# Head-wise weighted values in half-height tiles, with the sums of weights moved and inverted through DRAM

## What is computed

```
xn = _layernorm(x, axis=-1)
x = x + attn(xn, Wqkv, Wout) + ffn(xn, W1, b1, W2, b2)      # ffn: relu(xn W1 + b1) W2 + b2, 256 -> 1024 -> 256

# attn: H = 16 heads of hd = 16, segments of 512 tokens, keys are every 8th token of a segment (64 keys)
scores = jnp.einsum('bhspd,bhskd->bhspk', q4, k4)            # 512 x 64 for each head and segment
c = jnp.max(scores, axis=4, keepdims=True)                   # over blocks of 64 tokens, per key
w = jnp.exp(scores - c)
den = jnp.sum(w, axis=-1) + 1e-10
num = jnp.einsum('bhsnmk,bhskd->bhsnmd', w, v4)
out = num / den[..., None]                                   # then times Wout
```

## Time and profile before

| | |
|---|---|
| time, median of 3 runs | 1187.57 us (1187.46 to 1188.78) |
| profiled execution, span (the page gives no other time for it) | 1189.4 us |
| TensorE busy | 1162.9 us, 98% |
| VectorE busy | 885.6 us, 74% (reciprocals 222.3 us of it) |
| ScalarE, GpSimd busy | 657.1 us (55%), 613.5 us (52%) |
| 16 DMA engines | 32.6% |

### The profile page before, as it was taken

The page is one execution under the profiler, slowest core; times in us unless marked ns, Lnnn a source line. Parts: engine busy times, 40 slices in busy tenths (PEclk is TensorE's granted clock), DMA queues, the critical chain, the costliest instruction groups (busy, mean ns, idle before and its releaser), DMA issues.

```text
span 1189.4 us, 22871 instructions
## 1 busy us (share of the span) xinstructions
PE 1162.9 (98%) x7457; PEld 955.7 (80%) x7457; DVE 885.6 (74%) x1437; ACT 657.1 (55%) x1142; POOL 613.5 (52%) x488
## 2 busy tenths in 40 slices
PE   5799999999999999999999999999999999999998
PEld 3578888888878888888888888888888888888888
DVE  7788777778787777777777787777877777777762
ACT  4545555565655565555565555556555555555653
POOL 2435654465554455554556544556544556544554
PEclk9889999999999999999999999999999999999999
DMA  5423343222333322333222433223343233332210
GB/s 184 99 73 93 85 106 100 63 82 70 101 101 84 80 72 81 98 106 84 68 81 75 106 101 84 72 70 88 101 106 82 56 87 84 106 102 55 67 49 36
DMA packets 75402, 102.24 MB, mean 86 GB/s; under 512 B 13808, under 2 KB 42096, under 8 KB 75376
## 3 DMA queue, kind: packets, MB, share of 16 engines
q1 hardware_dynamic: 75376, 101.90, 32.6%
HBM read 22.16 MB, written 16.78 MB: 33 GB/s over the span
## 4 chain that ended last, share of the span: by engine, by line
PE 96%; DVE 1%; issue 0%; SPq 0%; POOL 0%; DMA 0%; ACT 0%; DVEq 0%; POOLq 0%
PE y_bank L690 39%; PE h_bank L690 38%; PE misc L811 5%; PE s_bank L742 5%; PE misc L814 5%; PE misc L756 2%; PE misc L690 2%; PE misc L781 0%; PE misc L764 0%; DMA q_pack<-q_hi 0%; PE s_bank L690 0%; DVE w_exp L589 0%; DVE s_max L583 0%; DVE xn_keys L544 0%; DVE w_lo L506 0%
## 5 line engine op out<-in xcount | busy, mean ns | idle before, releaser
L338 POOL TENSOR_TENSOR h_lo<-h_full,h_hi 128x512 fp32r<-128x512 f32 x256 | 336.7, 1318 | 557.2 <-ACT h_full L403 553.3
L409 ACT ACTIVATE w_exp<-w_exp 128x512 f32<-128x512 f32 x256 | 162.7, 636 | 238.7 <-DVE w_exp L589 238.7
L690 PE MATMUL y_bank<-w_hi,h_hi 128*128 128x256 f32 x1024 | 290.6, 284 | 0.0
L690 PE MATMUL y_bank<-w_lo,h_hi 128*128 128x256 f32 x1024 | 290.5, 284 | 0.0
L690 PE MATMUL y_bank<-w_hi,h_lo 128*128 128x256 f32 x1024 | 290.2, 283 | 0.0
L596 DVE RECIPROCAL den<-den 128x256 f32<-128x256 f32 x128 | 222.3, 1739 | 39.9 <-ACT den L422 39.9
L401 ACT ACTIVATE h_hi<-h_bank,b_cols 128x512 fp32r<-128x512 f32 x256 | 176.1, 688 | 82.6 <-PE h_bank L690 76.8
L690 PE MATMUL h_bank<-xt_hi,w_hi 128*128 128x512 f32 x512 | 210.8, 412 | 1.9 <-DVE q_lo L611 1.9
L690 PEld LDWEIGHTS y_bank<-w_lo,h_hi 128*128 128x128 f32 x1024 | 196.0, 191 | 9.9
L690 PEld LDWEIGHTS y_bank<-w_hi,h_hi 128*128 128x128 f32 x1024 | 195.5, 191 | 9.3
L690 PE MATMUL h_bank<-xt_lo,w_hi 128*128 128x512 f32 x512 | 201.9, 394 | 0.0
(11 more groups left out here) (91 smaller groups left out, 1708.1 us busy)
## 6 DMA issues: line engine op xcount, KB each, us to landing
q_pack<-q_hi SPq DMA_DIRECT2D x256, 128.0 KB, 2.4
x_raw<-x SPq DMA_DIRECT2D x32, 512.0 KB, 3.3
q_pack<-q_lo SPq DMA_DIRECT2D x128, 128.0 KB, 2.4
out<-y SPq DMA_DIRECT2D x32, 512.0 KB, 2.9
k_pack<-k_hi SPq DMA_DIRECT2D x256, 32.0 KB, 1.9
k_pack<-k_lo SPq DMA_DIRECT2D x128, 32.0 KB, 1.9
x_keys<-x SPq DMA_DIRECT2D x16, 128.0 KB, 3.0
w_exp<-w SPq DMA_DIRECT2D x2, 1024.0 KB, 8.8
```

The lines of the kernel that those rows point to most:

```text
L338: pool.tensor_tensor(h_part[1][:, i % HBUF], h_full[:, i % HBUF], f32(h_part[0][:, i % HBUF]), ALU.subtract).then_inc(h_lo, 1)
L409: act.activation(w_exp[:, pair], w_exp[:, pair], ACT.Exp).then_inc(w_ready, 1)
L690: mm = pe.matmul(ps, stationary[a], moving[b], start=start and c == 0 and n == 0, stop=stop and c == len(pairs) - 1 and n == 2, skip_group ...
```

## The change

The change computes the same. Weighted values and sums of weights come out of one set of products: `v` holds for each pair 32 columns in which values and ones alternate, and each head has a product of its own, with its 64 keys as rows and 32 columns: 8 products for a quad, head a = 0 of the pairs into `misc[0]` and a = 1 into `misc[1]`. So every second row of a bank is a value row, and the others all hold a sum. ACT takes both banks in one copy of 128 x 1024. SP moves one sum row of each head (4 rows a bank) to DRAM and reads them back as 128 x 64; DVE adds 1e-10 and inverts that; SP writes it to DRAM again and reads it back into the 64 rows of each half in four DMAs; another DMA merges the value rows of the second bank into the first. POOL multiplies. Wout is loaded with its rows in the new order, in four DMAs. Cut to its core:

```diff
-        v = sb("v", [P, 2, D], F32)
+        v = sb("v", [P, 2, PAIRS, PW], F32)
...
@@ SyncE
+            def move_den(s):
+                sp.wait_ge(num_den_ready, (s + 1) * QUADS)
+                for a in range(2):
+                    sp.dma_start(den_dram[:, :, a].rearrange("q j n -> j q n"),
+                                 num_den[1 - a::PW, :, a]).then_inc(den_out, 16)
+                sp.wait_ge(den_out, (s + 1) * 32)
+                sp.dma_start(den[:], den_dram.rearrange("q j a (c n) -> (q j a c) n", c=P // H)).then_inc(den_in, 16)
+                sp.dma_start(num_den[1::2, :, 0], num_den[1::2, :, 1]).then_inc(num_merged, 16)
+            def move_rden(s):
+                sp.wait_ge(rden_ready, s + 1)
+                sp.dma_start(rden_dram.rearrange("q j a (c n) -> (q j a c) n", c=P // H), rden[:]).then_inc(rden_out, 16)
+                sp.wait_ge(rden_out, (s + 1) * 16)
+                for quad in range(QUADS):
+                    for a in range(2):
+                        sp.dma_start(rden_rows[a::2, quad],
+                                     rden_dram[quad, :, a].unsqueeze(1).to_broadcast([P // PW, HD, SEG])
+                                     ).then_inc(rden_rows_in, 16)
             def step(s, par, ffn, attention, norm, load):
+                if ffn:
+                    move_rden(s)
                 if load:
...
                 if norm:
                     pack(s)
+                if attention:
+                    move_den(s + 1)
                 if ffn:
                     sp.wait_ge(y_ready, (s + 1) * YB)
@@ GpSimd
             def attention_out(s, quad):
-                pool.wait_ge(rden_ready, (s * QUADS + quad + 1) * (RP // QUADS))
-                pool.wait_ge(num_ready, s * QUADS + quad + 1)
+                pool.wait_ge(rden_rows_in, (s + 1) * 64)
+                pool.wait_ge(num_merged, (s + 1) * 16)
...
-                    if i in (4, 6) and ffn:
-                        attention_out(s, i // 2 - 2)
-                    if i in (5, 7) and ffn:
-                        attention_lo(s, i // 2 - 2, par)
+                    if i in (6, 7) and ffn:
+                        attention_out(s, i - 6)
+                if ffn:
+                    for quad in range(QUADS):
+                        attention_lo(s, quad, par)
@@ ScalarE
-                act.copy(num[:, quad], misc[0][:]).then_inc(num_ready, 1)
-                act.add(den[:, quad], misc[1][:], GUARD).then_inc(den_ready, 1)
+                act.copy(num_den[:, quad], misc_banks[:]).then_inc(num_den_ready, 1)
...
-                    if i == 5 and ffn:
-                        attention_hi(s, 0, par)
...
                 if ffn:
+                    attention_hi(s, 0, par)
+                if attention:
+                    exponential(s, PAIRS - 2)
+                if ffn:
                     attention_hi(s, 1, par)
-                if attention:
-                    exponential(s, PAIRS - 2)
@@ VectorE
-                dve.reciprocal(den[:, quad, columns], den[:, quad, columns]).then_inc(rden_ready, 1)
+            def invert_den(s):
+                dve.wait_ge(den_in, (s + 1) * 16)
+                dve.tensor_scalar(den[:], den[:], GUARD, None, ALU.add).then_inc(den_guarded, 1)
+                dve.wait_ge(den_guarded, s + 1)
+                dve.wait_ge(rden_out, past(s * 16))
+                dve.reciprocal(rden[:], den[:]).then_inc(rden_ready, 1)
...
-                    if n in (2, 4) and ffn:
-                        invert_den(s, RP // QUADS + n // 2 - 1)
+                    if n == 2 and ffn:
+                        invert_den(s)
...
@@ TensorE, weighted_values
-                for j, pair in enumerate(pairs):
-                    pe.matmul(misc[0][PW * j:PW * (j + 1), :], v[:, 1 - par, PW * pair:PW * (pair + 1)],
-                              w_exp[:, pair], start=True, stop=True)
-                for j, pair in enumerate(pairs):
-                    mm = pe.matmul(misc[1][PW * j:PW * (j + 1), :], head_ones[:], w_exp[:, pair],
-                                   start=True, stop=True)
+                for j in range(PAIRS // QUADS):
+                    pair = quad * (PAIRS // QUADS) + j
+                    for a in range(2):
+                        rows = slice(a * KEYS, (a + 1) * KEYS)
+                        mm = pe.matmul(misc[a][PW * j:PW * (j + 1)], v[rows, 1 - par, pair], w_exp[rows, pair],
+                                       start=True, stop=True)
```

More of the change, by code:

```diff
@@ L128, in bank @@
             return ctx.enter_context(nc.psum_tensor(name, [P, SEG], F32))
-        misc = [bank(f"misc{i}") for i in range(2)]
+        misc_banks = ctx.enter_context(nc.psum_tensor("misc", [P, 2, SEG], F32))
+        misc = [misc_banks[:, i] for i in range(2)]
         h_bank = [bank(f"h_bank{i}") for i in range(2)]
@@ L180, in ln_attention_ffn @@
         pv_psum = sem("pv_psum")
-        num_ready = sem("num_ready")
-        den_ready = sem("den_ready")
+        num_den_ready = sem("num_den_ready")
+        den_out = sem("den_out")
+        den_in = sem("den_in")
+        den_guarded = sem("den_guarded")
+        num_merged = sem("num_merged")
+        rden_out = sem("rden_out")
+        rden_rows_in = sem("rden_rows_in")
         rden_ready = sem("rden_ready")
@@ L267, in first_step @@
                 sp.dma_start(w2_raw, w2.rearrange("(c p) n -> p c n", p=P)).then_inc(w2_loaded, 16)
-                sp.dma_start(wout_raw, wout_t.rearrange("(c p) n -> p c n", p=P)).then_inc(w2_loaded, 16)
+                wout_heads = wout_t.rearrange("(c j a d) n -> c a j d n", c=DH, a=2, d=HD)
+                for c in range(DH):
+                    for a in range(2):
+                        sp.dma_start(wout_raw[a::2, c], wout_heads[c, a]).then_inc(w2_loaded, 16)
                 sp.dma_start(b1_cols[:], b1).then_inc(const_loaded, 16)
@@ L341, in attention_out @@
             def attention_out(s, quad):
-                pool.wait_ge(rden_ready, (s * QUADS + quad + 1) * (RP // QUADS))
-                pool.wait_ge(num_ready, s * QUADS + quad + 1)
+                pool.wait_ge(rden_rows_in, (s + 1) * 64)
+                pool.wait_ge(num_merged, (s + 1) * 16)
                 pool.wait_ge(att_hi, past((s - 1) * QUADS + quad + 1))
-                pool.tensor_tensor(att[:, quad], num[:, quad], den[:, quad], ALU.mult).then_inc(att_ready, 1)
+                pool.tensor_tensor(att[:, quad], num_den[:, quad, 0], rden_rows[:, quad], ALU.mult).then_inc(att_ready, 1)
             def attention_lo(s, quad, par):
@@ L705, in first_product, with first_product_chunk, second_product @@
                     pe.wait_ge(h_ready, n - 1)
-                three_products(h_bank[i % 2][:],
-                               [([w[:, c, i * P:(i + 1) * P] for w in w1s], [x_[:, par, c] for x_ in xt])
-                                for c in range(DH)], True, True).then_inc(h_psum, 1)
-            def second_product(s, i):
+            def first_product_chunk(i, par, c):
+                return three_products(h_bank[i % 2][:],
+                                      [([w[:, c, i * P:(i + 1) * P] for w in w1s], [x_[:, par, c] for x_ in xt])],
+                                      c == 0, c == DH - 1)
+            def first_product(s, i, par, attention=True):
+                first_product_waits(s, i, attention)
+                for c in range(DH):
+                    mm = first_product_chunk(i, par, c)
+                mm.then_inc(h_psum, 1)
+            def second_product(s, i, tokens=range(T)):
                 n = s * NH + i
@@ L713, in second_product @@
                     pe.wait_ge(w_lo, len(splits))
-                pe.wait_ge(h_hi, n + 1)
-                pe.wait_ge(h_lo, n + 1)
-                for t in range(T):
+                if 0 in tokens:
+                    pe.wait_ge(h_hi, n + 1)
+                    pe.wait_ge(h_lo, n + 1)
+                for t in tokens:
                     if i == 0 and t % 2 == 0:
@@ L797, in queries, with weighted_values_waits @@
                                True, True).then_inc(q_psum, 1)
-            def weighted_values(s, quad, par, norm):
+            def weighted_values_waits(s, quad, norm):
                 pe.wait_ge(v_ready, (s + 2) * 2)
```

72 lines of the change are left out of this document (39 added, 33 removed).

## The result

The changed kernel takes 1232.18 us in the median of 4 runs (1230.93 to 1235.92), the kernel before beside it 1188.17: a ratio of 1.0379 (95% interval 1.0362 to 1.0395), 3.8% slower. The likeliest case, a chain of DMAs longer than a step, is the one that came, and the time lies in both ranges; but the forecast was 22 us more than before and the result is 44 us more.

The account below looks back on a forecast made before the run. A DMA chain from `pack` to `pack` was to bind: 36.5 us a round, 30 rounds from 62.8 to 1157.8; step 30 19.2 late plus 3.7 gave span 1212, so 1210 us (1188 to 1236; all cases 1135 to 1240).

Parts of the forecast that it names:

- The likeliest case: The DMA chain binds and is longer than a step: 1210 us, own range 1188 to 1236, chance 0.55.
- step 5: Four DMAs broadcasting the inverses from DRAM back to 64 rows each: 7.4 us on four engines, 4.6 if shared over 16.
- steps 1 to 4: From the end of `pack`: sums to DRAM, read back, DVE's guard and inversion, out to DRAM again; done at X+8.2.
- steps 6 and 7: POOL's multiplications and `h_lo` of tile 7, 3.9 us; then ACT's `att_hi` and `k_hi` and DVE's `k_lo`, 1.7 us.
- TensorE spared: Quad products on TensorE: eight tiles at once, two rounds instead of four, saving 0.87 us a quad, 56 for 64 quads.
- The chain binds: DMA chain from `pack` to `pack` takes 36.5 us a round against TensorE's 34.2; TensorE waits 2.3 us a step.
- The narrow end: Broadcasts of the inverses shared out by their four source rows, so four DMA engines do all: 7.4 us.
- The first `pack` of the count: Start of the sum over 30 rounds: the first `pack` was put as ending at 62.8.
- The wait that I named: In step 30, TensorE's second product of tile 7 waits 5.4 us for `h_lo`; less 1.7 saved gives 3.7.
- The rival *wide: Broadcasts run wide and TensorE stays the bound: round 33.7 us, 1130 to 1160 us, middle 1145; chance 0.27.
- Shorter hops: Narrow chain with landings of 1.8 and earlier moving: round 34.2 to 35.8, 1145 to 1187 us; chance 0.07 faster, 0.04 same.
- Moving at pack's rate: Broadcast rows move at 14 GB/s an engine: round 40.8 us, total 1340; chance 0.05 together with a falling clock.

Follow-up runs that it names:

- wide: Changed kernel with new layout of both DRAM arrays and the broadcasts (32 rows by 1024 columns each, source repeated 16 times outermost): 1149.74 us, ratio 0.9666.
- half: Changed kernel with only quad 0's two broadcasts made (256 KB instead of 512) and both quads multiplied by them: 1159.12 us, ratio 0.9764.
- mid: Changed kernel with the sums' DMAs issued in the middle of `pack`, narrow broadcasts and ACT's order kept: 1202.99 us, ratio 1.012.
- dose: Changed kernel with the sums read back from DRAM twice, the second read behind the landing of the first: 1331.94 us, ratio 1.1201.

## Why the prediction was right in kind and low in size

The chain, its links and the direction were right. What failed is the size of one link, step 5, the broadcasts back (8.9 us for 7.4), and the path at the end of the program (60.6 us for 54.2). An error the other way in steps 1 to 4 took back most of the first.

The terms of the sum, as means over the 27 rounds from the fourth on (us, between starts in the timelines; X is the end of `pack`):

| | prediction | changed | wide | half | mid | dose |
|---|---|---|---|---|---|---|
| X to the first `rden_rows` issue (steps 1 to 4) | 8.2 | 6.95 | 7.0 | 7.0 | 3.4 | 10.1 |
| from there to POOL's `att` (step 5) | 7.4 | 8.9 | 5.0 | 6.1 | 9.0 | 8.95 |
| to the first k DMA (steps 6 and 7) | 5.6 | 5.4 | 6.7 | 5.9 | 5.4 | 5.4 |
| k DMAs to the first q DMA | 1.9 | 2.2 | 2.1 | 2.2 | 2.2 | 2.2 |
| to the end of `pack` | 13.4 | 13.5 | 13.5 | 13.5 | 16.2 | 13.5 |
| round | 36.5 | 36.9 | 34.3 | 34.6 | 36.1 | 40.2 |

In wide TensorE has the round (83% of the chain), and the third line holds slack: 6.7 for 5.4. In half it is 5.9; there the loop and TensorE are nearly equal.

**TensorE spared: right.** 0.84 a quad for 0.87. **The chain binds: right**, and shown twice over: two cuts at different places free the kernel, a dose lengthens each round, and TensorE's work can be given back for nothing.

**Steps 1 to 4: forecast too long by 1.2.** The two small landings of DRAM that a row now shows are 1.7 (`den`) and 1.8 (`rden_dram`), under the 1.9 that I had set as lower bound; I took 2.1 for each. DVE's two instructions on 128 x 64 took 0.20 (guard) and 0.55 us (inversion), as forecast. The page's DMA issues:

```profile
den<-den_dram SPq DMA_DIRECT2D x32, 32.0 KB, 1.7
rden_dram<-rden SPq DMA_DIRECT2D x32, 32.0 KB, 1.8
x_raw<-x SPq DMA_DIRECT2D x32, 512.0 KB, 7.3
```

**Step 5: the mis-sized term, forecast too short by 1.5.** "420 GB/s are 26 for one engine, so 512 KB take 5.0, and with 2.4 it is 7.4". The rows moved at 88 to 92 GB/s and not at 105, so 512 KB take 5.8, and x's 512 KB, of which I had only looked at their own delay, are issued before the rows are in: `x_raw` lands after 7.3 us instead of 3.3, and the hop is 8.9. In the round shown above x's bytes come while the rows are still under way: the share is 1.02 for a while and then falls back to 0.24, before POOL starts at 594.41:

```profile
591.00:591.50 0.50, 0.50 (x4) 0.41 (x3) 0.00 (x0) 0.00 (x0) 0.00 (x0) 1.00 1.02 393
592.50:593.00 0.50, 0.50 (x6) 0.50 (x5) 0.50 (x1) 0.50 (x2) 0.00 (x0) 1.00 0.24 78
```

The narrow end was the right choice between the two. My reason for it, that a piece of work is cut where both sides can be cut, was an argument and no measurement; what the runs show is a share of 0.24 for these four rows and of 0.80 for wide's layout. How the 1.5 divide between the rate (0.8 by these numbers) and x's load is only worked out, not measured apart.

**The round is 0.4 longer than forecast: these two errors and three of 0.1 to 0.3 in the other lines.** That the sum came so near is luck: 1.5 too little and 1.2 too much nearly cancel, and with step 5 alone put right the round would have been 38.0 and the time about 1255 (an estimate: 30 x 1.5 more). Even so the round is the larger part of the miss. The mean of 30 rounds, the first ones at 37 to 38.5 among them, is 36.99, which over 30 rounds is 14.8 us more than 36.5. The first `pack` of the count ends at 60.0 and not 62.8: 2.8 less.

**The end of the program: 6.4 short.** From the last `pack` on I had 54.2 (1212 less 1157.8), and it is 60.6 (1230.4 less 1169.8). The wait that I named is there, and is 6.0 for 5.4. Timeline of TensorE, and windows around it and over the last 8.4 us:

```profile
1188.91 0.55 PE L728 MATMUL y_bank<-w_hi,h_hi 128*128 128x256 f32 x1 [5.98 <-POOL h_lo L376]
...
1221.95 0.36 PE L728 MATMUL y_bank<-wout_hi,att_hi 128*128 128x256 f32 x1 [2.04 <-POOL att_lo L388]
```

```profile
1183.00:1191.70 8.70, 2.79 (x12) 2.64 (x12) 1.35 (x2) 2.30 (x4) 5.43 (x5) 0.62 0.06 23
...
1222.00:1230.40 8.40, 4.56 (x24) 4.35 (x24) 1.38 (x2) 0.00 (x0) 0.00 (x0) 0.75 0.16 62
```

I had missed two things. Both `att_lo` now stand behind POOL's last `h_lo` (2.0 us in the last step, where only `output_product` is left). And the granted clock was 0.50 for a part of both windows (from 1186 to 1191.7, and from 1223 to 1226), behind idle stretches: 0.62 and 0.75 on average, where the same work of the kernel before has 1.00 (1149 to 1158, and 1177.0 to 1185.4). In the last one products follow at 0.21 instead of 0.12, 1.4 us more; in the other 1.2. With the inverses at X+16.4 instead of X+15.6 this makes 0.8 + 2.0 + 1.4 + 1.2 = 5.4 of the 6.4; the last 1.0 I have not traced.

**The rest is the scale.** The profiled execution's span is 1230.4 and its time 1232.2, the median; before, the median lay 1.8 below the profiled span, and I had carried that over: 3.6. In all runs here the time is 1.8 us above the span of the same execution (1.74 to 2.03), so the execution that was profiled before was some 3 us longer than the usual one; its later first `pack` (the 2.8 above) may be part of the same, which is not shown. Together: 14.8 - 2.8 + 6.4 + 3.6 = 22.0, the whole miss.

**The error bar and the rivals.** I had given the round 0.8 of error, and it was 0.4 off; the change in time is the small difference of a round of 36.9 and a step of 35.9, so 0.4 in the round is nearly as much again as the 0.6 that I had forecast. The rival *wide* was the right alternative: made real, it gives 1149.7, where I had 1145. What I put down for it, that all transfers of the trace run at the full rate, was too much: in the earlier trace rows `out` and `x_raw` have 420 GB/s, `pack` 202 at a share of 0.89. *Shorter hops* was half true and outweighed by step 5. *Moving at pack's rate* is out: 14 GB/s an engine, against the 23 and 24 of the two windows (88 and 92 GB/s at a share of 0.24). Two slips stand in the ranges: the lower end of all, 1135, was called the middle of the wide case's span, which is 1145, and the 1340 of *moving at pack's rate* lies outside the range of all.

## What to carry to other kernels

When a small result is sent through DRAM, add up the whole way from the queue's last work in one step to its last work in the next; if that way passes through the same in-order queue, it is a loop, and its length is a floor for the step however much slack each engine has. Look for the link that is in the loop only by its place in an engine's list: here the high part of the keys, which needs nothing of the sums, stood behind one that does, and moving it was worth 68 us, giving the broadcasts another shape 82. When the balance between loop and engine is a few tenths of a microsecond a step, the loop may tell the sign, but the size is then uncertain by as much as itself.

## What the runs showed of the hardware

- A broadcast DMA whose source has four different rows as slowest dimension kept the share of the 16 DMA engines at 0.24, with 88 to 92 GB/s; the same bytes with 16 repeats outermost had 0.80 and 205 GB/s, and each such DMA landed after 2.8 us in the median.
- DMAs of 32 KB from and to DRAM landed after 1.7 and 1.8 us; within SBUF the 32 KB of `pack` took 1.9.
- The granted clock fell behind waits inside the program too. In the changed kernel TensorE was busy 3.84 of the 6 us from 555 to 561, and from 561 to 565 the granted clock was 0.63 (0.50 from 561 to 563, 0.53 in the next 1 us, then 1.00); over the span it is 0.982 (0.993 before), in dose 0.953. That it costs little in the middle rounds, where TensorE isn't what the loop waits for, is argued and not shown.

```profile
555.00:561.00 6.00, 3.84 (x19) 3.00 (x19) 2.07 (x3) 1.36 (x3) 3.04 (x3) 0.96 0.26 86
561.00:565.00 4.00, 4.00 (x30) 2.73 (x30) 1.86 (x4) 2.49 (x6) 3.34 (x3) 0.63 0.04 8
```
